# Sorting edge records by source: PE matmuls in 13 groups and 221 chunk writes in place of 832 single-record writes

## The chip, the core and the metric

The kernel runs on one core of one Trainium2 chip. The metric is the device time in microseconds of one execution, from the first to the last instruction with what lies around it; the median of three runs stands for a kernel. Engines: PE (TensorE, with PEld for its weight loads), DVE (VectorE), ACT (ScalarE), POOL (GpSimd), SP (SyncE, which here only issues DMAs).

## What is computed

Four layers of a graph network over 6250 nodes with 128 features and 106,250 edges that are sorted by destination, each followed by a residual sum and a layer norm. The layers, cut to what matters:

```python
x = ln(x + mean_by_dst(x[src]) @ W_neigh.T + b)                        # neighbour mean
x1 = relu(mean_by_dst(x[src]) @ Wl + x @ Wr + b)                       # sage 1
x_sage = relu(mean_by_dst(x1[src]) @ Wl2 + x1 @ Wr2 + b2)              # sage 2
x_gat = relu(attention over dst, 2 heads, of (x_sage @ W)[src])        # gat
x_rgcn = means by (dst, kind of edge) of (x_gat @ Wrel)[src]; x = ln(x + normalize(concat @ Wf))
ef = concat(x[row], x[col], edge_attr); h = relu(batch_norm(ef @ W1 + b1))
x = ln(x + x + segment_sum(h @ W2 + b2, row) / (count + 1))            # sums by SOURCE (row = src)
x = ln(x + (x @ W0 + segment_sum(h8[edge_type, src] * weight, dst)) / degree)
```

The edges come sorted by destination. The third layer sums by source, so the kernel needs, for every edge, a record (low part of the source, destination, two attributes) at a place that is ordered by source.

## The kernel before

**Tiles and passes.** 128 edges are a tile; T = 832 tiles, in turns of U = 16. `aggregate` is one pass over all edges, and runs six times: `block0`, `sage1`, `sage2`, `gat`, `rgcn` and, at the end, a last one. In each, POOL issues one gather per tile (L378) of the rows of the tile's sources into one of 16 message buffers; DVE builds a 128 x 128 matrix with a one for each edge at its destination's place in the window (L389, L392: the hot, made eight tiles ahead); PE multiplies the two into one of eight PSUM windows (L569, each f32 matmul stands as two records; in `block0` a second one, L572, gives the degree); DVE adds the window to the accumulator (L485). PE begins a half of eight windows only when DVE has added the half before, POOL refills a half's buffers only when PE has used them, and DVE reads a half's eight window bases into registers at its start. Each engine keeps the order in which its code is written. In `block0` two windows share a PSUM bank, and DVE's add of the first of a pair waits for PE's second; in the other passes each window has its own bank.

**Between the passes** lie the node stages `after_block0`, `after_sage1`, `after_sage2`, `after_gat` and `after_rgcn`, and `attention_terms` and `attention_softmax` between `sage2` and `gat`. Each is a block: every engine must end its part before any engine starts the next.

**Placing the edges.** In `block0` DVE also finds each edge's place in the order by source: 13 turns count how many edges of each partition fall in each of 49 blocks of sources (`count_block`, L397, a row of 832 elements each), PE sums these, and 49 times DVE masks a block, scans it for ranks and copies them (`mask_block` L402, `rank_block` L406, `place_block` L423). The table of places is `m.position`. Then POOL writes all records to DRAM with indirect DMAs, one for each tile, each of 128 records of 16 bytes: 108 in `after_block0`, 42 with `sage1` and its node stage, 165 with `sage2` and its stage, 240 in `attention_terms`, 107 in `attention_softmax`, 83 and 87 with `gat` and `rgcn` and theirs (`PLACES`; `Records`, L628, and `place_records`, L603). In `after_rgcn` SP waits for all of them (`load_when`) before it loads the first block of records, and its remaining stores of node rows stand behind that.

**By source.** `edge_hidden` gathers again, T2 = 880 tiles in the new order (L2001), and `scatter_by_source` sums them (loads at L2139). T2 is larger than T because each block of sources is filled up to whole tiles.

## Time and profile before

| what | value |
|---|---|
| median of 3 runs | 9341.97 us (9337.46 to 9349.73) |
| span of the profiled execution | 9347.3 us |
| busy: PE, DVE, ACT, POOL | 6289.6, 4856.4, 1137.4, 6808.7 us |
| mean granted PE clock, share of full | 0.68 |
| six passes over the edges | 1040 to 1052 us each |

A row of the busy table by stretches gives a stretch of the span, its length, and for each engine its busy time with the number of its records, then the granted clock of PE as a share of its upper level, the busy share of the DMA engines and their rate. A row of a timeline gives start, length, engine, line, operation and what ended the idle time before it. A group gives count, busy time and mean length of one, then the idle time of the engine ahead of these and its causes.

### The profile page before, as it was taken

The page shows a single profiled execution, that of the slowest core. Times are in us where ns is not written, and L with a number is a line of the kernel's source. Part 1 is how long each engine was busy: PE and PEld are TensorE (multiplying, and loading weights), DVE is VectorE, ACT ScalarE, POOL GpSimd, SP SyncE. Part 2 cuts the span into 40 slices and gives each one's busy share as a digit, 9 for nine tenths or more (in the row PEclk, how much of TensorE's full clock was granted, in tenths as well). Part 3 has the DMA queues.
Part 4 walks back from the last instruction along what each step waited for, and adds up shares of the span by engine and source line. Part 5 has one row for each costly group of instructions (what it writes and reads, how often), then busy time and mean ns, then how long its engine had stood idle before and what let it go on. Part 6 is the DMA issues. An engine that isn't in the chain of part 4 may idle for free. (4 is left out here: it accounts for less than half of the span.)

```text
span 9347.3 us, 137432 instructions
## 1 busy us (share of the span) xinstructions
PE 6289.6 (67%) x30105; PEld 4833.2 (52%) x30105; DVE 4856.4 (52%) x16305; ACT 1137.4 (12%) x2570; POOL 6808.7 (73%) x7484
## 2 busy tenths in 40 slices
PE   5666646666777789907888856665566658866665
PEld 5555424444566655607777644443455557634443
DVE  7776634444555535757777544445222217644445
ACT  0000100000000005800000100001222227610000
POOL 6777777777777777777777777777677767457775
PEclk7777755555666687559999955556777779965555
DMA  3212112222333332006777522212777765421211
GB/s 88 53 52 52 49 47 53 53 53 63 115 105 105 105 99 59 2 13 202 222 221 222 175 58 52 52 52 58 172 191 192 193 167 155 151 94 53 53 52 53
DMA packets 666147, 935.83 MB, mean 100 GB/s; under 512 B 276164, under 2 KB 445164, under 8 KB 665500
## 3 DMA queue, kind: packets, MB, share of 16 engines
q0 software_dynamic: 271328, 605.65, 24.3%
q1 hardware_dynamic: 295136, 324.43, 11.1%
q10 hardware_dynamic: 99548, 4.42, 0.9%
q14 instruction: 108, 0.88, 0.0%
q8 instruction: 27, 0.44, 0.0%
HBM read 790.93 MB, written 143.03 MB: 100 GB/s over the span
## 5 line engine op out<-in xcount | busy, mean ns | idle before, releaser
L569 PE MATMUL sage_window<-sage_hot,sage_message 128*128 128x128 f32 x4992 | 1438.7, 427 | 756.2 <-DMA sage_message<-t_x,all_src 315.1
L569 PEld LDWEIGHTS sage_window<-sage_hot,sage_message 128*128 128x128 f32 x4992 | 1067.3, 291 | 1127.8 <-issue 793.0
L378 POOL DMA_INDIRECT block_message<-t_rel,all_src x832 | 786.7, 946 | 424.1 <-issue 253.3
L485 DVE TENSOR_TENSOR first_acc<-first_acc,sage_window 128x128 f32 (+1 forms) x1664 | 590.4, 355 | 953.8 <-PE sage_window L569 946.8
L2001 POOL DMA_INDIRECT eh_message<-t_q,all_position x880 | 832.9, 946 | 278.1 <-issue 266.8
L378 POOL DMA_INDIRECT block_message<-in_x,all_src x832 | 791.6, 951 | 287.1 <-issue 253.0
L378 POOL DMA_INDIRECT gat_message<-t_h,all_src x832 | 791.8, 952 | 263.9 <-issue 253.0
L569 PE MATMUL gat_window<-gat_hot,gat_message 128*128 128x128 f32 x6656 | 845.7, 281 | 205.1 <-DVE gat_hot L389 116.3
L378 POOL DMA_INDIRECT sage_message<-t_x,all_src x832 | 786.4, 945 | 264.4 <-issue 253.2
L378 POOL DMA_INDIRECT rgcn_message<-t_rel,all_src x832 | 786.9, 946 | 262.1 <-issue 253.3
L378 POOL DMA_INDIRECT sage_message<-t_s,all_src x832 | 788.3, 948 | 259.9 <-issue 253.3
L569 PEld LDWEIGHTS gat_window<-gat_hot,gat_message 128*128 128x128 f32 x6656 | 782.4, 192 | 264.5 <-issue 142.8
L569 PE MATMUL block_window<-block_hot,block_message 128*128 128x128 f32 x1664 | 638.3, 487 | 409.7 <-DMA block_message<-t_rel,all_src 330.4
L569 PE MATMUL rgcn_window<-rgcn_hot,rgcn_message 128*128 128x128 f32 x1664 | 613.9, 479 | 362.3 <-DMA rgcn_message<-t_rel,all_src 296.9
L2058 PE MATMUL eh_ps<-eh_hot,eh_window 128*128 128x128 f32 x1760 | 466.3, 357 | 413.9 <-DMA eh_message<-t_q,all_position 394.0
L569 PEld LDWEIGHTS block_window<-block_hot,block_message 128*128 128x128 f32 x1664 | 416.5, 311 | 632.1 <-issue 440.1
L569 PE MATMUL block_windows<-block_hot,block_message 128*128 128x128 f32 x1664 | 482.7, 384 | 381.1 <-DVE first_acc L485 161.3
L569 PEld LDWEIGHTS rgcn_window<-rgcn_hot,rgcn_message 128*128 128x128 f32 x1664 | 415.1, 314 | 556.6 <-issue 400.3
L2031 DVE TENSOR_SCALAR_CACHE_REDUCE eh_hot<-eh_low_rows,all_column 128x128 f32<-128x128 bf16 x880 | 243.7, 342 | 857.4 <-DMA eh_low_rows<-t_low 857.1
L2058 PEld LDWEIGHTS eh_ps<-eh_hot,eh_window 128*128 128x128 f32 x1760 | 363.6, 256 | 486.3 <-issue 474.9
L569 PEld LDWEIGHTS block_windows<-block_hot,block_message 128*128 128x128 f32 x1664 | 360.0, 268 | 461.0 <-DVE block_hot L392 235.4
L392 DVE TENSOR_SCALAR sage_hot<-all_iota,all_rel 128x128 f32<-128x128 f32 x1680 | 498.4, 298 | 149.1 <-issue 149.0
(430 smaller groups left out, 10992.8 us busy)
## 6 DMA issues: line engine op xcount, KB each, us to landing
eh_window<-t_p SPq DMA_DIRECT2D x880, 64.0 KB
t_hidden<-eh_hidden SPq DMA_DIRECT2D x110, 512.0 KB
sc_rows<-t_hidden SPq DMA_DIRECT2D x110, 512.0 KB, 3.6
eh_low_rows<-t_low SPq DMA_DIRECT2D x110, 256.0 KB
t_rel<-n_h SPq DMA_DIRECT2D x49, 512.0 KB, 2.6
eh_message<-t_q,all_position POOLq DMA_INDIRECT x880
block_message<-in_x,all_src POOLq DMA_INDIRECT x832, 2.5
sage_message<-t_x,all_src POOLq DMA_INDIRECT x832, 2.5
```

Source lines behind the costliest of these rows:

```text
L378: pool.indirect_dma_start(message[u][:], None, table, bass.IndirectOffsetOnAxis(ap=index[:, it * U + u:it * U + u + 1], axis=0)).then_inc( ...
L392: ins = nc.vector.tensor_scalar(hot[:, u, :], m.iota[:], m.rel[:, t], None, ALU.is_equal)
L485: nc.vector.tensor_tensor(window, window, ps[k], ALU.add).then_inc(e.window_used, 1)
L569: last = nc.tensor.matmul(ps[k][:, b, :], message[u][:, f:f + P], hot[:, u, j * P:(j + 1) * P], start=(j == 0), stop=(j == heads - 1))
L2001: pool.indirect_dma_start(message[:, u, :], None, m.t_q, bass.IndirectOffsetOnAxis(ap=m.dst[:, it * U + u:it * U + u + 1], axis=0)).then_i ...
L2031: nc.vector.tensor_scalar(hot[:, q, e], rows, m.column[:], 0.0, ALU.is_equal, ALU.add, accum_out=m.of_source[:, bass.ds(it * U + q * QU + ...
L2058: nc.tensor.matmul(ps[q][:, e], window[:, u, :], hot[:, q, e], start=False, stop=False, skip_group_check=True)
```

## The change

The rank of an edge is found and used in another way.

- In `block0`, class `EdgeSlots` replaces the mask, scan and copy. The tiles are cut in G = 13 groups of 64. In the first 13 turns DVE compares, for eight tiles at a time, the sources' blocks with 0 to 48 (`hit`, 392 elements, bf16) and PE sums that over the partitions (`add_up`); `keep` copies the counts out. `find_starts` turns them into a first place for each group and block, once. In the remaining 39 turns (three for each group, 48 slots) DVE and PE rank eight tiles in six slots: `hit`, a matmul with a triangle, a product that picks each edge's rank, a sum over the blocks, and a matmul with the complement. The slots 0 to 23 of a group hold further steps, among them one scan and three operations on 850 elements.
- In `sage1`, class `EdgeSort` moves the records themselves. For four tiles (a quad) DVE makes in slot 4q two comparisons, `high_hot` (272 elements) and `low_hot` (512), and in slot 4q+1 the product `masked` (1088: one-hots of 68 places times four-word records). In slot 4q+3 PE multiplies them in four f32 matmuls of 272 columns (`move`), and 64 tiles make one group's sum, which DVE takes out (`keep`). The windows of `sage1` now lie in pairs in a bank, as in `block0`, which frees a bank for the sums.
- POOL then writes chunks of four records: 17 for each group, 221 in all, 51 with `sage1` and its node stage and 170 with `sage2` and its stage (four of each at the end of the pass). ACT copies ten groups out of the way in `after_sage1`. The writes, their loads and their waits in all other stages are gone.
- T2 is 896, since every group's part of a block is filled up to whole chunks. The clearing of tables is cut in seven DMAs.

```diff
-T2 = 880
+T2 = 896
...
+G = 13
+GT = T // G
+TURNS = GT // U
+BT = 8
+BATCHES = GT // BT
+CHUNK = 4
+SPAN = 68
+CHUNKS = SPAN // CHUNK
...
+WRITES = {"sage1": (0, 3 * CHUNKS), "sage2": (3 * CHUNKS, G * CHUNKS)}
+EARLY_CHUNKS = 4
...
-            if records and not places_edges:
-                pool.wait_ge(weights_in, 16 * len(loads))
-                records.write_early(pool)
+            if sorts:
+                pool.wait_ge(sort.kept, 1)
+            if chunks:
+                chunks.write_early(pool)
...
-                    if part == "count" and u % 4 == 1:
-                        count_block(it * 4 + u // 4)
...
+                    if counts is not None and u % 2 == 0:
+                        order.count(dve, counts, u // 2)
+                    if ranks is not None:
+                        order.rank(dve, ranks[0], ranks[1] * U + u)
+                    if of_sort is not None:
+                        sort.spread(dve, of_sort[0], of_sort[1] * U + u)
                     one_hot(bass.ds(it * U + u + HU, 1), (u + HU) % U)
-                    last_of_bank = u | 1 if places_edges else u
+                    last_of_bank = u | 1 if paired else u
...
+                if counts is not None:
+                    order.keep(dve, counts)
+                if of_sort is not None and of_sort[1] == TURNS - 1:
+                    sort.keep(dve, of_sort[0])
...
+                    if counts is not None and u % 2 == 1:
+                        order.add_up(pe, counts, u // 2)
+                    if ranks is not None:
+                        order.rank_up(pe, ranks[0], ranks[1] * U + u)
+                    if of_sort is not None:
+                        sort.move(pe, of_sort[0], of_sort[1] * U + u)
...
+    def hit(self, dve, tiles, k, used):
...
+        dve.wait_ge(self.hit_used[k], used)
...
+        self.nc.vector.tensor_tensor(self.hits[:, k], keys, blocks, ALU.is_equal).then_inc(self.hit_ready[k], 1)
...
+    def add_up(self, pe, g, i):
...
+        pe.wait_ge(self.hit_ready[k], g * (BATCHES // 2) + i // 2 + 1)
+        self.nc.tensor.matmul(self.ps_count[:, 0:BT * NT], self.ones[:], self.hits[:, k].rearrange("p j b -> p (j b)"), start=(i == 0),
+                              stop=(i == BATCHES - 1), skip_group_check=True).then_inc(self.hit_used[k], 1)
...
+    def rank(self, dve, n, s):
...
+        if role == 0:
+            self.hit(dve, n * GT + i * BT, k, n * half + i // 2 + G * half)
...
+        if role == 3:
+            dve.wait_ge(self.ranked, n * BATCHES + i + 1)
+            ranks = self.ps_rank[:, 0:BT * NT].rearrange("p (j b) -> p j b", b=NT)
+            tt(self.picked[:], ranks, self.hits[:, k], ALU.mult).then_inc(self.picked_ready, 1)
+        if role == 4:
+            dve.wait_ge(self.picked_ready, n * BATCHES + i + 1)
+            nc.vector.tensor_reduce(self.slot[:, bass.ds(n * GT + i * BT, BT)], self.picked[:], AX.X, ALU.add)
...
+        if role == 1:
+            pe.wait_ge(self.hit_ready[k], n * half + i // 2 + 1 + G * half)
+            nc.tensor.matmul(out, self.before[:], hits, start=False, stop=True, skip_group_check=True).then_inc(self.ranked, 1)
+        if role == 4:
+            pe.wait_ge(self.picked_ready, n * BATCHES + i + 1)
+            nc.tensor.matmul(out, self.rest[:], hits, start=False, stop=True, skip_group_check=True).then_inc(self.hit_used[k], 1)
...
+        if role == 0:
+            dve.wait_ge(self.used[k], n * (quads // 2) + q // 2)
+            tt(self.high_hot[:, k], places(SPAN), key(self.high, SPAN), ALU.is_equal).then_inc(self.hots_ready, 1)
+            tt(self.low_hot[:, k], places(P), key(self.low, P), ALU.is_equal).then_inc(self.ready[k], 1)
+        if role == 1:
+            dve.wait_ge(self.hots_ready, n * quads + q + 1)
...
+            tt(self.masked[:, k], hot, rows, ALU.mult).then_inc(self.ready[k], 1)
...
+    def move(self, pe, n, s):
...
+        if role == 3:
...
+            pe.wait_ge(self.ready[k], n * quads + q // 2 * 2 + 2)
+            for t in range(QU):
+                last = self.nc.tensor.matmul(self.ps[:, 0:SPAN * REC], self.low_hot[:, k, t], self.masked[:, k, t].rearrange("p h k -> p (h k)"),
+                                             start=(q == 0 and t == 0), stop=(q == quads - 1 and t == QU - 1), skip_group_check=True)
...
-        @block.gpsimd
-        def _(pool):
-            records.write(pool, 0, records.count)
-            records.settle(pool)
...
-                    order.load_when(sp, records)
+                    order.load(sp, 0)
```

PE in `sage1`, at the start of a turn. Before, the third and the following windows:

```order
L569 MATMUL sage1_window2<-sage1_hot,sage1_message2 128x128 [waits all_gathered2,all_hot_ready]
L564 REGISTER_ALU
L569 MATMUL sage1_window3<-sage1_hot,sage1_message3 128x128 [waits all_gathered3,all_hot_ready]
L564 REGISTER_ALU
L569 MATMUL sage1_window4<-sage1_hot,sage1_message4 128x128 [waits all_gathered4,all_hot_ready]
```

The same place in the change (`sage1_sort_ready0` counts DVE's `low_hot` and `masked`):

```order
L536 MATMUL sage1_windows1<-sage1_hot,sage1_message2 128x128 [waits all_gathered2,all_hot_ready]
L795 ISA [waits sage1_sort_kept]
L797 MATMUL sage1_ps_sort<-first_acc,sage1_sort_low_hot 128x272 [waits sage1_sort_ready0]
L797 MATMUL sage1_ps_sort<-first_acc,sage1_sort_low_hot 128x272 x3
L531 REGISTER_ALU
L536 MATMUL sage1_windows1<-sage1_hot,sage1_message3 128x128 [waits all_gathered3,all_hot_ready]
```

Four sorting matmuls and their waits have come between the windows of messages 2 and 3, which share the bank `sage1_windows1`.

DVE in `sage1`, at the same tiles. Before, from the first window's add to the second's:

```order
L485 TENSOR_TENSOR first_acc<-first_acc,sage1_window0 128x128
L392 ISA
L392 TENSOR_SCALAR sage1_hot<-all_iota,all_rel 128x128
L479 REGISTER_ALU
L481 REGISTER_ALU [waits all_window_ready]
L485 ISA [waits all_window_used]
L485 TENSOR_TENSOR first_acc<-first_acc,sage1_window1 128x128
```

In the change, from the first window's add on:

```order
L458 TENSOR_TENSOR first_acc<-first_acc,sage1_windows0 128x128
L784 ISA
L787 ISA [waits sage1_sort_hots_ready]
L787 TENSOR_TENSOR first_acc<-sage1_sort_high_hot,first_acc 128x1088
L399 ISA
L399 TENSOR_SCALAR sage1_hot<-all_iota,all_rel 128x128
L454 REGISTER_ALU [waits all_window_ready]
```

The product `masked` (written into the unused half of `first_acc`) stands ahead of the second add; the add of the third window, a few rows on, waits for the fourth.

PE in `block0`, in the turns that count. Before and in the change, from the second matmul of the first window (`setup_dst_in` stands for `hit_ready`, since semaphores' names are used again):

```order
L572 MATMUL block0_windows0<-block0_hot,all_ones 128x128
L564 REGISTER_ALU
L569 MATMUL block0_windows0<-block0_hot,block0_message1 128x128 [waits all_gathered1,all_hot_ready]
L572 MATMUL block0_windows0<-block0_hot,all_ones 128x128
L564 REGISTER_ALU
```

```order
L539 MATMUL block0_windows0<-block0_hot,all_ones 128x128
L609 ISA [waits setup_dst_ready,setup_ea_in]
L610 MATMUL block0_ps_count<-block0_hits,block0_ones_b 128x392 [waits setup_dst_in]
L531 REGISTER_ALU
L536 MATMUL block0_windows0<-block0_hot,block0_message1 128x128 [waits all_gathered1,all_hot_ready]
L539 MATMUL block0_windows0<-block0_hot,all_ones 128x128
```

A counting matmul with a wait for DVE stands ahead of every second window.

## Rows read from the trace of the kernel before

**Rows 1.** busy time by stretches: us; PE, PEld, DVE, ACT, POOL; clock, DMA share, GB/s:
```profile
33.00:1085.00 1052.00, 675.71 (x3324) 595.95 (x3324) 764.51 (x1938) 0.00 (x0) 791.62 (x832) 0.72 0.22 57
...
1239.00:2279.00 1040.00, 633.95 (x1660) 415.30 (x1660) 430.33 (x1669) 0.00 (x0) 786.25 (x832) 0.50 0.21 55
...
2344.00:3386.00 1042.00, 801.00 (x3320) 649.50 (x3320) 550.74 (x1668) 0.00 (x0) 788.32 (x832) 0.65 0.37 107
...
3620.00:4000.00 380.00, 342.37 (x2720) 220.38 (x2720) 277.81 (x633) 314.77 (x628) 286.61 (x288) 0.50 0.04 7
...
4222.00:5272.00 1050.00, 889.65 (x7024) 823.05 (x7025) 819.16 (x2650) 0.00 (x0) 791.93 (x833) 0.99 0.76 220
```

**Rows 2.** groups of the second pass (line, engine, form, count | busy us, mean ns | idle):
```profile
L378 POOL DMA_INDIRECT sage_message<-t_x,all_src x832 | 786.4, 945 | 264.4 <-issue 253.2 <-ACTq L325 11.1
...
L569 PE MATMUL sage_window<-sage_hot,sage_message 128*128 128x128 f32 x1660 | 634.2, 487 | 505.7 <-DMA sage_message<-t_x,all_src 313.8 <-DVE sage_hot L392 112.3 <-DVE first_acc L485 77.6
```

**Rows 3.** timeline (start us, length us) at the end of the first node stage:
```profile
1143.61 0.19 DVE L823 TENSOR_SCALAR all_has_edges<-n_degree 128x49 f32<-128x49 f32 x1
...
1238.82 0.34 SPq L353 DMA_DIRECT2D weights_sage_wl<-in_L_gnn_sage_Wl  x1
```

**Rows 4.** timeline, end of the attention terms and first instruction of the softmax:
```profile
3964.62 0.20 ACT L1204 COPY attention_e<-al_picked 128x8 f32<-128x8 f32 x1 [1.26 <-DVE al_picked L1243]
...
3993.80 0.36 SPq L1439 DMA_DIRECT2D softmax_spread<-t_last  x1
```

**Rows 5.** timeline of the softmax: the table's store and POOL's first gather of it:
```profile
4122.71 0.35 SPq L1441 DMA_DIRECT2D t_self<-softmax_spread  x1
...
4154.90 0.98 POOL L1434 DMA_INDIRECT softmax_rows<-t_self,all_last_edge  x1 [1.40 <-DMA t_rec<-attention_records,all_position]
```

**Rows 6.** timeline of the node stage behind the relational pass: SP's load, DVE's next:
```profile
6548.62 0.33 SPq L2497 DMA_DIRECT2D all_src_high<-t_rec  x1
...
6562.31 0.69 DVE L1867 TENSOR_TENSOR second_acc<-n_ps,second_fused_bias 128x512 f32<-128x512 f32 x1 [39.00 <-DMA t_q<-second_acc]
```

**Rows 7.** the node stage behind the second pass: POOL's writes, next stage's first DMA:
```profile
L628 POOL DMA_INDIRECT t_rec<-weights_records_sage,all_position x42: 966/972/1016, 2279.5 to 2336.7; - x42
...
2343.71 0.37 SPq L353 DMA_DIRECT2D first_sage_wl<-in_L_gnn_sage_Wl  x1
```

**Rows 8.** groups that go by T2: the gathers, and the loads behind them:
```profile
L2001 POOL DMA_INDIRECT eh_message<-t_q,all_position x880 | 832.9, 946 | 278.1 <-issue 266.8
...
L2139 SPq DMA_DIRECT2D sc_rows<-t_hidden x110: 332/333/343, 7726.8 to 8071.3; - x110
```

**Rows 9.** DVE forms by width:
```profile
L1261 DVE TENSOR_TENSOR al_product<-al_ps,al_high_hot 128x392 f32<-128x392 f32 x46 | 26.0, 566 | 21.9 <-issue 13.9 <-PE al_ps L1278 7.9
...
L1075 DVE TENSOR_TENSOR n_product<-first_sage_wg,first_sage_att 128x512 f32<-128x512 f32 x4 | 2.8, 688 | 0.1
...
565.60 1.09 DVE L498 TENSOR_TENSOR all_x<-all_x,neigh_neigh_bias 128x896 f32 x1
```

**Rows 10.** timeline of PE pairs at half clock (first pass) and full clock (node stage):
```profile
570.45 0.63 PE L569 MATMUL block_windows<-block_hot,block_message 128*128 128x128 f32 x2
...
570.87 0.63 PE L572 MATMUL block_windows<-block_hot,all_ones 128*128 128x128 f32 x2
...
571.65 0.42 DVE L485 TENSOR_TENSOR first_acc<-first_acc,block_windows 128x256 f32 x1 [1.24 <-PE block_windows L572]
...
2336.93 0.59 PE L912 MATMUL n_ps<-weights_sage_wl,first_acc 128*128 128x256 f32 x2
...
2337.36 0.59 PE L913 MATMUL n_ps<-weights_sage_wr,n_x_t 128*128 128x256 f32 x2
```

**Rows 11.** timeline of DVE in the second pass:
```profile
1503.31 0.30 DVE L392 TENSOR_SCALAR sage_hot<-all_iota,all_rel 128x128 f32<-128x128 f32 x1 [1.08 <-issue]
...
1503.62 0.29 DVE L485 TENSOR_TENSOR first_acc<-first_acc,sage_window 128x128 f32 x1
...
1503.83 0.52 DVE L392 TENSOR_SCALAR sage_hot<-all_iota,all_rel 128x128 f32<-128x128 f32 x1
```

More of the change, by code:

```diff
@@ L890, in _ @@
         def _(pool):
-            records.write_rest(pool)
+            chunks.write_rest(pool)
         @block.tensor
@@ L964, in by_half, with after_sage2 @@
     return weights.rearrange("(b k) n -> k b n", k=P)
[L967 removed]
+def after_sage2(nc, m, a, w, chunks):
     with ExitStack() as ctx:
@@ L989, in _ @@
         def _(pool):
-            records.write_rest(pool)
+            chunks.write_rest(pool)
         @block.sync
```

439 lines of the change are left out of this document (268 added, 171 removed).

## The prediction

> **What bounds the kernel now.** I read the busy table by stretches first [rows 1]. POOL has the same 786 to 792 us of work in every pass over the edges, and each such pass lasts 1040 to 1052 us, whatever PE and DVE do in it. The groups of the second pass say why: 832 gathers, 945 ns each, and 253 us of issue time between them [rows 2]; (786.4 + 253.2) / 832 = 1.25 us for one tile, so 5.00 us for four tiles and 20.0 us for sixteen. PE stands idle there for 314 us because a gathered tile has not landed. So a pass is paced by POOL, and DVE (430 of 1040 us in the second pass, 765 of 1052 us in the first) and PE (634 and 676 us) have room. What counts is whether they keep it. Between the passes POOL sets the time too wherever it still writes records while the other engines have ended [rows 3 to 7].
>
> **What goes away.** The 832 record writes cost POOL 972 ns and some 0.30 us of issue each (42 of them in 57.2 us, with the barrier at their start, 1.39 us each [rows 7]). Only those that stand alone are worth time; I go by the seams.
> - First node stage: DVE's last instruction ends at 1143.8, the next pass begins at 1238.8 [rows 3]; 108 writes fill the gap. With no POOL work in the stage, the last store of node rows must land and the engines meet; I allow 4 us. Gain 91 us.
> - Attention terms: the last copy ends at 3964.8, the softmax starts at 3993.8 [rows 4]. Gain 27 us after 2 us for the meeting.
> - Softmax: the table is stored at 4122.71 + 0.35, and some 2 us later it can be gathered; POOL starts only at 4154.90, after its 107 writes [rows 5]. Gain 30 us; the 49 gathers and DVE's end follow as they are.
> - Node stage behind the relational pass: SP's load of the sorted records is queued behind the wait for all writes, ahead of the stores of node rows; DVE stands for 39.0 us on such a store [rows 6]. With the records long written, what is left is the load itself and the stores behind it. Gain 32 us.
> - Node stage behind the attention pass: other work ends within 7 us of the writes; gain 6 us, an estimate from the same kind of seam.
> Together 186 us less.
>
> **What the 221 writes cost.** 51 stand in the stage where 42 stood: nine more at 1.28 us, and there the stage's last activation ends near the writes, so 12 us are added; the next stage now starts at 2343.7 [rows 7]. I take 13. 170 stand where 165 stood, beside PE work that ends last: 4 us. ACT's three copies of sorted rows stand ahead of its first copy in the second node stage and are covered by those writes.
>
> **T2 from 880 to 896.** Sixteen more gathers at (832.9 + 278.1) / 880 = 1.26 us give 20 us [rows 8]; the loads behind come at (8071.3 - 7726.8) / 109 = 3.16 us for eight tiles, so 6 us. Together 26 us. All these small terms: -186 + 13 + 4 + 26 = **-143 us**.
>
> **What the second pass gains in work.** Per four tiles DVE gets three products of 272, 512 and 1088 elements. DVE takes 566 ns for 392, 688 ns for 512 and 1.09 us for 896 elements [rows 9], about 1.04 ns for each further one: so 0.44, 0.69 and 1.29 us. PE gets four f32 matmuls of 272 columns, each two records. At the lower of its two levels, 1.2 GHz, two records of 128 columns are 0.42 us apart (570.45 to 570.87); at 2.4 GHz two of 256 columns take 0.43 us [rows 10]. Four times 272 columns: 3.57 us at the lower level, 1.83 us at the upper one.
>
> Taken as sums they fit: DVE's four hots and adds (0.52 us a pair [rows 11]), half of a base read of 1.08 us and 2.3 us of new work make 4.9 us of 5.00, and PE has 2.7 to 5.3 us. But they don't run side by side. The order of the rows on PE shows the four sorting matmuls ahead of the window 4q+3 and behind a wait for the masked records of the same four tiles. DVE makes these in its slot 4q+1, and its next add, of window 4q+2, needs window 4q+3, because both lie in one bank. So each of the 208 quads has a loop in it:
> - PE: wake-up 0.08, sorting 1.83 or 3.57, the pair of window 4q+3 0.21 or 0.42, and 0.36 from the pair's last start plus its share to DVE's add (571.29 to 571.65 [rows 10]): 2.5 or 4.4 us, in which DVE has only two hots and an add to do;
> - DVE from there, in starts 0.21 and 0.31 us behind each other [rows 11]: add, hot, add 0.73; the products of 272 and 512, overlapped, 0.97; hot and add 0.52; the product of 1088 in full 1.29; half a base read 0.54: 4.05 us.
> One turn is **6.5 us** at the upper level and **8.5 us** at the lower, against POOL's 5.00.
>
> Which level? PE would work 5.4 of 8.5 us, 63%. In the rows 61% goes with a granted 0.50, 90% (the attention terms) with 0.50 too, 77% with 0.65, 85% with 0.99, and the first pass, where PE works in lumps, has 0.72 at 64% [rows 1]. Here PE works in lumps of up to 5 us, so I take a quarter of the time at the upper level: 1 / (0.25 / 6.5 + 0.75 / 8.5) = 7.9, rounded to 7.8 us. 208 x 7.8 = 1622 us. Ahead of it DVE waits for the records, which SP loads behind the weights and eight clearing stores, 22 us in which no add is done; the 13 moves of a group's sum out of PSUM add 5. The pass lasts 1649 us instead of 1040: **+609 us** (bounds +339 and +755). The Trainium skill (TensorE: Matmul & The Clock Gate, "A second HAM failure mode: psum-queue depth-cycling") says that short idles between groups of matmuls make the clock alternate; the 0.65 and 0.72 of the rows are such mixtures, and by that the turn would lie between the two levels, as taken.
>
> **What the first pass gains in work.** It loses 49 blocks of mask, scan and copy and 52 counts, and gets two parts.
> - Counting, 13 turns of 16 tiles. Every second window DVE makes a product of 392 elements (0.57 us), PE adds it up ahead of the next window, and DVE's add waits for that window, again for the bank. At the lower level: 0.57 + 0.08 + matmul 0.33 (bf16, an estimate at half the f32 price per column) + two pairs 0.84 + 0.36 + add 0.34 + hot 0.31 + add 0.34 = 3.17, with a quarter of a base read 3.44; eight of them and 1.2 us for keeping the counts make 28.7 us against 20.0. At the upper level 24.1. PE works in small pieces there, so mostly the lower: +100 us (53 to 112).
> - Ranking, 39 turns or 104 batches of six windows, against 7.5 us of POOL. DVE: six hots and adds 3.9, three operations on 392 elements 1.45, three quarters of a base read 0.8, and 0.8 for the group's scan and its three products of 850 elements; the two places where DVE waits on PE behind a matmul of the ranking add 0.5 us at the upper level and 2.7 at the lower. So 7.4 to 9.65 us a batch: 0 to +222 us; at the first pass's 0.72 [rows 1] nearer to the upper end than PE's share suggests, since DVE now waits at every batch: +155.
> - The starts are found in some 30 linked steps, once: +10.
> Together **+265 us** (bounds +60 and +345).
>
> **Long loops.** The bodies are three and four turns long, 26 passes in all. A base read at a loop's start now shows 1.08 us of idle [rows 11]; a pass over a longer body may cost nothing more or up to the 6 us of a seam [rows 7]: 0 to 150, taken at 26. The Trainium skill (Runtime: NRT & Kernel Launch, "Instruction fetch mechanics") says that an engine holds two pages of instructions and that a taken branch out of them waits for a fetch; no row here shows that price, and by the upper bound the sum would be some 120 us more.
>
> **Sum.** The profiled span is 9347 us, the median of the runs 9342, so I add to the median: 9342 - 143 + 609 + 265 + 26 = 10099, **10100 us**.
>
> **Rivals.**
> - *The passes keep POOL's pace.* For it: the sums of work fit, and POOL is up to 16 tiles ahead. Against it: the loop of waits above, which no lead of POOL shortens. It decides at 5.00 us a quad, where PE's part would have to vanish behind DVE's. Then 9342 - 143, and 22 for the late start: some 9220 us, faster by 1.3%. Chance 0.09.
> - *The loop binds, but PE runs at the upper level throughout.* The 0.99 of the attention pass speaks for it, its 85% against it. 9342 - 143 + 339 + 60 = 9600 us. Chance 0.17.
> - *The lower level throughout, and costly loops.* 9342 - 143 + 755 + 345 + 50 to 100: 10350 to 10400 us. Chance 0.13.
> - *The writes are not fewer, or not off the seams.* 13 groups of 17 chunks are 221 and all stand in two stages, so no more than a little of the 186 us is open; it decides nothing here. A product of 1088 elements read through two repeated patterns could be dearer than its length: each 0.3 us is 62 us.
> The forecast has 0.61.
>
> **Range.** From the second rival with a little off its seams, 9560, to the third, 10370 us. A measurement tells 0.2% (19 us) from no change. Faster than that 0.09, within it 0.02, slower 0.89.
>
> **What would show it.** In the second pass: POOL's idle waits for PE's window (none now) of some 600 us; DVE's adds waiting on window records in each quad; starts of the masked product 7 to 8.5 us apart; granted clock 0.6 to 0.7. The first pass 1250 to 1400 us long, with a counting turn of 24 to 29 us. The stage behind it some 60 us instead of 154, the attention terms and softmax 57 us shorter together. It is wrong if DVE's product of 1088 elements and PE's sorting overlap, if the turn is under 5 us, or if the clock stands at 0.9 or more.

## The result and the profile after

The changed kernel takes 10110.73 us (median of 4 runs, 10102.03 to 10127.92) against 9340.4 us for the kernel before on the same chip: 1.0825 times as long, 95% interval 1.0809 to 1.0840. The forecast was 10100 us. The profiled execution spans 10105.8 us, 758.5 us more than the 9347.3 us of before.

Where the time went is read best from POOL's gathers, since each pass begins with one and ends soon after one. These are the rows of the gathers' line in the changed kernel: shortest, median and longest in ns, then the start of the first and of the last in us.

```profile
L384 POOL DMA_INDIRECT block_message<-in_x,all_src x832: 938/944/1837, 33.5 to 1363.2; - x167
L384 POOL DMA_INDIRECT sage_message<-t_x,all_src x832: 938/944/1897, 1435.3 to 3100.2; - x167
L384 POOL DMA_INDIRECT sage_message<-t_s,all_src x832: 942/946/1002, 3190.8 to 4230.0; - x167
L384 POOL DMA_INDIRECT gat_message<-t_h,all_src x832: 940/946/1082, 5015.3 to 6061.0; - x167
L384 POOL DMA_INDIRECT rgcn_message<-t_rel,all_src x832: 940/944/1008, 6168.2 to 7206.1; - x167
L384 POOL DMA_INDIRECT block_message<-t_rel,all_src x832: 940/944/1064, 9007.7 to 10045.3; - x167
L2172 POOL DMA_INDIRECT eh_message<-t_q,all_position x896: 940/944/1177, 7311.1 to 8434.1; - x180
```

The same rows of the kernel before:

```profile
L378 POOL DMA_INDIRECT block_message<-in_x,all_src x832: 939/946/1804, 33.0 to 1083.5; - x167
L378 POOL DMA_INDIRECT sage_message<-t_x,all_src x832: 940/945/1065, 1239.5 to 2278.2; - x167
L378 POOL DMA_INDIRECT sage_message<-t_s,all_src x832: 942/947/1005, 2344.4 to 3385.0; - x167
L378 POOL DMA_INDIRECT gat_message<-t_h,all_src x832: 942/949/1049, 4222.9 to 5270.6; - x167
L378 POOL DMA_INDIRECT rgcn_message<-t_rel,all_src x832: 940/945/1006, 5391.2 to 6430.4; - x167
L378 POOL DMA_INDIRECT block_message<-t_rel,all_src x832: 940/945/1160, 8247.7 to 9286.8; - x167
L2001 POOL DMA_INDIRECT eh_message<-t_q,all_position x880: 940/945/1124, 6584.1 to 7684.0; - x176
```

Their differences give each stage, first gather to last for a pass, last to first for what lies between:

| stretch | before, us | after, us | change | forecast |
|---|---|---|---|---|
| first pass | 1050.5 | 1329.7 | +279 | +265 |
| first node stage | 156.0 | 72.1 | -84 | -91 |
| second pass | 1038.7 | 1664.9 | +626 | +609 |
| node stage behind it | 66.2 | 90.6 | +24 | +13 |
| second sage stage, attention terms, softmax | 837.9 | 785.3 | -53 | -53 |
| node stage behind the attention pass | 120.6 | 107.2 | -13 | -6 |
| node stage behind the relational pass | 153.7 | 105.0 | -49 | -32 |
| edge network's gathers, and the loads behind | 1663.6 | 1696.6 | +33 | +26 |
| the four other passes | 4166.6 | 4160.4 | -6 | 0 |
| long loops, counted apart | | | inside the passes | +26 |

The sum is +757 against the spans' +758.5. The difference is rounding and the stretches ahead of the first gather and behind the last. (The -53 forecast is -27 -30 for the two seams and +4 for the chunks in that stretch.)

Three groups of the second pass answer to [rows 2] (line, engine, form, count | busy us, mean ns | idle us and what ended it):

```profile
L384 POOL DMA_INDIRECT sage_message<-t_x,all_src x832 | 813.5, 978 | 923.6 <-PE sage_windows L536 629.9
L797 PE MATMUL sage_ps_sort<-first_acc,sage_sort_low_hot 128*128 128x272 f32 x1664 | 732.1, 613 | 540.5 <-DVE first_acc L787 540.5
L458 DVE TENSOR_TENSOR first_acc<-first_acc,sage_windows 128x128 f32 x832 | 236.6, 284 | 739.6 <-PE sage_windows L536 739.6
```

POOL waited for nobody here before; now it waits 629.9 us for windows of PE. PE waits 540.5 us for DVE's masked records, and DVE 739.6 us for PE's windows. Two engines that each wait for the other, with neither full, are the picture of a loop. One turn of it, from the timeline (start us, length us, engine, line, idle before):

```profile
1499.88 0.29 DVE L458 TENSOR_TENSOR first_acc<-first_acc,sage_windows 128x128 f32 x1 [2.02 <-PE sage_windows L536]
...
1502.60 1.28 DVE L787 TENSOR_TENSOR first_acc<-sage_sort_high_hot,first_acc 128x1088 f32<-128x1088 f32 x1
...
1503.93 3.99 PE L797 MATMUL sage_ps_sort<-first_acc,sage_sort_low_hot 128*128 128x272 f32 x8 [2.19 <-DVE first_acc L787]
...
1507.72 1.92 PE L536 MATMUL sage_windows<-sage_hot,sage_message 128*128 128x128 f32 x8
...
1508.59 0.29 DVE L458 TENSOR_TENSOR first_acc<-first_acc,sage_windows 128x128 f32 x1 [4.11 <-PE sage_windows L536]
```

DVE adds at 1499.88, its product starts at 1502.60, PE sorts from 1503.93, the windows follow, and DVE's next add comes at 1508.59, after 4.11 us of waiting. The next product stands at 1510.56: 7.96 us for four tiles, where POOL needs 5.00. The eight sorting records took 3.99 us here and 2.10 us in the quad at 1497.33, which are the two levels of PE's clock, 1.2 and 2.4 GHz.

### The profile page after: what moved, and what is told of

It is laid out like the page before. It is cut to its first block and busy times, and to the rows that moved or that the text cites. A ratio compares the mean times of both kernels' runs of the same rounds, so it can differ in the third digit from the quotient of the medians.

```text
span 10105.8 us, 143547 instructions
## 1 busy us (share of the span) xinstructions
PE 6830.9 (68%) x32219; PEld 5310.8 (53%) x32219; DVE 5317.0 (53%) x17381; ACT 1149.4 (11%) x2599; POOL 6251.9 (62%) x6901
## 5 line engine op out<-in xcount | busy, mean ns | idle before, releaser
L384 POOL DMA_INDIRECT sage_message<-t_x,all_src x832 | 813.5, 978 | 923.6 <-PE sage_windows L536 629.9
L384 POOL DMA_INDIRECT block_message<-in_x,all_src x832 | 815.1, 980 | 543.3 <-PE block_windows L539 290.1
L797 PE MATMUL sage_ps_sort<-first_acc,sage_sort_low_hot 128*128 128x272 f32 x1664 | 732.1, 613 | 540.5 <-DVE first_acc L787 540.5
L384 POOL DMA_INDIRECT block_message<-t_rel,all_src x832 | 785.3, 944 | 426.1 <-issue 253.2
L536 PE MATMUL sage_window<-sage_hot,sage_message 128*128 128x128 f32 x3328 | 807.5, 399 | 252.3 <-DMA sage_message<-t_s,all_src 114.3
L536 PEld LDWEIGHTS sage_window<-sage_hot,sage_message 128*128 128x128 f32 x3328 | 654.5, 282 | 405.4 <-issue 247.8
L797 PEld LDWEIGHTS sage_ps_sort<-first_acc,sage_sort_low_hot 128*128 128x128 f32 x1664 | 470.9, 296 | 709.6 <-DVE first_acc L787 585.7
L458 DVE TENSOR_TENSOR first_acc<-first_acc,sage_windows 128x128 f32 x832 | 236.6, 284 | 739.6 <-PE sage_windows L536 739.6
L458 DVE TENSOR_TENSOR first_acc<-first_acc,block_windows 128x256 f32 x832 | 350.1, 421 | 436.2 <-PE block_windows L539 432.4
```

The source lines that it names most:

```text
L384: pool.indirect_dma_start(message[u][:], None, table, bass.IndirectOffsetOnAxis(ap=index[:, it * U + u:it * U + u + 1], axis=0)).then_inc( ...
L458: nc.vector.tensor_tensor(window, window, ps[k], ALU.add).then_inc(e.window_used, 1)
L536: last = nc.tensor.matmul(ps[k][:, b, :], message[u][:, f:f + P], hot[:, u, j * P:(j + 1) * P], start=(j == 0), stop=(j == heads - 1))
L797: last = self.nc.tensor.matmul(self.ps[:, 0:SPAN * REC], self.low_hot[:, k, t], self.masked[:, k, t].rearrange("p h k -> p (h k)"), start= ...
```

## Experiments on the loops

**The sorting a quad late.** A quad is four tiles. PE's sorting matmuls of quad q-1 stand where those of quad q stood, and the last quad of a group is sorted behind it.

```diff
-        if role == 3:
+        due = [q - 1] if role == 3 and q > 0 else []
+        if s == GT - 1:
+            due = due + [q]
+        for q in due:
+            k = q % 2
```

> The changed kernel, with one thing moved: in the second pass PE sorts the quad q-1 (not q) ahead of window 4q+3, and the last quad of a group behind it. The work and the output stay. Theory (the loop of waits): the masked records are then made some six slots before PE wants them, nothing in a quad waits for its own products, and the quad falls from 8.03 us to POOL's 5.0, at most 5.4 where PE is full at the lower level. The pass lasts 1060 to 1130 us instead of 1665, the kernel 9490 to 9570 us, about 9530; POOL's wait for PE's windows in it falls from 630 us to under 80. Rival (the amount of work, or the two engines disturbing each other): the same instructions run, so the time stays at 10110, within 40 us.

**The sorting a slot late.** The same with `role == 0`: quad q-1 is sorted ahead of window 4q.

> The changed kernel, with PE's sorting of quad q put one slot later: ahead of window 4q+4 instead of ahead of window 4q+3. The work and the output stay. Theory (the loop): DVE then has an add, a hot, an add and the next quad's two hots of 272 and 512 elements to do beside the sorting. From one masked product to the next: 1.28 + sorting 3.57 + two windows 0.84 + 0.36 + the add's start 0.21 = 6.3 us at the lower level; at the upper one 4.1, so POOL's 5.0. With both, 5.8 to 6.1 instead of 8.03: 9640 to 9720 us, about 9680. Rival (the amount of work): 10110, within 40 us.

**One sorting matmul of four.**

```diff
-            for t in range(QU):
+            for t in range(1):
                 last = self.nc.tensor.matmul(self.ps[:, 0:SPAN * REC], ...
```

> The changed kernel with three of the four sorting matmuls of each quad left out (three quarters of the edges are then missing from the order by source and its stages compute with blank records); DVE makes all its products as in the changed kernel, and PE sorts in the same place. Theory (the loop): the turn loses 2.7 us at the lower level or 1.4 at the upper: 5.1 to 5.8 instead of 8.03, the kernel 9560 to 9680 us, about 9610. Rival (DVE's added products bound the pass by their amount): no change, 10110 within 40 us.

Measured: 9609.86 us a quad late and 9625.06 us a slot late, beside 9344.67 us for before. Both give back the better part of the loss with every instruction still there, so the amount of work is not what bound the pass. The granted clock in it rose as well, from 0.70 to 0.85 and 0.89, and these two runs can't tell how much of the gain is the clock's. With one matmul of four the kernel took 10003.71 us, but 369 us of that lie behind the relational pass (2171 us from its last gather to the last pass, against 1802 us with the sorting a quad late), where blank records are worked on; the second pass itself fell as foretold, at a clock of only 0.55, with its masked products 5.7 us apart in the mean. The gathers of the second pass, in this order a quad late, a slot late and one of four:

```profile
L384 POOL DMA_INDIRECT sage_message<-t_x,all_src x832: 942/948/2044, 1417.4 to 2604.7; - x167
...
L384 POOL DMA_INDIRECT sage_message<-t_x,all_src x832: 940/945/2021, 1444.9 to 2635.6; - x167
...
L384 POOL DMA_INDIRECT sage_message<-t_x,all_src x832: 942/947/1895, 1425.7 to 2625.8; - x167
```

The pass lasts 1187, 1191 and 1200 us instead of 1665. From the first I had expected 1060 to 1130 us and from the kernel 9490 to 9570, and it stopped short of both; the second came out a little under its 9640 to 9720. The groups of the gathers say why, in the same order:

```profile
L384 POOL DMA_INDIRECT sage_message<-t_x,all_src x832 | 929.6, 1117 | 324.0 <-issue 253.0 <-ACTq L329 65.4 <-PE sage_windows L536 5.5
...
L384 POOL DMA_INDIRECT sage_message<-t_x,all_src x832 | 923.4, 1110 | 336.5 <-issue 250.8 <-ACTq L329 68.3 <-PE sage_windows L536 17.4
...
L384 POOL DMA_INDIRECT sage_message<-t_x,all_src x832 | 834.5, 1003 | 434.6 <-issue 224.1 <-PE sage_windows L536 142.7 <-ACTq L329 67.8
```

With the sorting a quad late POOL's wait for windows is gone (5.5 us), its issue time is the old 253 us, but a gather takes 1117 ns instead of 945: 832 x 0.172 = 143 us, and 1039 + 143 = 1182. POOL sets the pace again, at a slower pace of its own; a slot late it is nearly the same. With one matmul of four the pass has a similar length for another reason: the loop is shorter but still there, POOL waits 142.7 us for windows, and its gathers are held back less (1003 ns).

**What holds a gather back.** In the timeline of the kernel with the sorting a quad late the long gathers are those that begin inside DVE's product:

```profile
1508.57 1.29 DVE L787 TENSOR_TENSOR first_acc<-sage_sort_high_hot,first_acc 128x1088 f32<-128x1088 f32 x1
...
1509.12 1.57 POOL L384 DMA_INDIRECT sage_message<-t_x,all_src  x1 [0.30 <-issue]
...
1519.78 1.28 DVE L787 TENSOR_TENSOR first_acc<-sage_sort_high_hot,first_acc 128x1088 f32<-128x1088 f32 x1
...
1520.00 1.89 POOL L384 DMA_INDIRECT sage_message<-t_x,all_src  x1 [0.30 <-issue]
```

Both end 0.83 us behind the product (1509.86 and 1510.69; 1521.06 and 1521.89), wherever in it they began, and so do all 205 that begin in one, 0.81 to 0.85 us behind it: a gather waits until the product is done and then needs most of its time. Of the pass's 832 gathers, 205 begin in a product of 1088 elements and take 1464 ns in the mean, 86 in one of 512 (1205 ns), 62 in one of 272 (1141 ns), 92 in a hot (954 ns) and 131 in an add out of PSUM (952 ns); 243 begin with DVE idle (946 ns). Against 946 ns the three products make 106 + 22 + 12 = 140 of the 143 us.

I tested this apart from sorting, in the kernel before, with one idle DVE operation for every four tiles of the second pass. Nothing waits for its result.

```diff
+                    if phase == "sage1" and u % 4 == 1:
+                        nc.vector.tensor_tensor(spare_out[:], spare_in[:], spare_in[:], ALU.mult)
                     one_hot(bass.ds(it * U + u + HU, 1), (u + HU) % U)
```

> The kernel before with one thing added in the second pass: once per four tiles, DVE multiplies one idle tile of 1088 elements by itself (two inputs in SBUF) into another that nobody reads. No loop is made, PE gets nothing, and DVE has room: 430 us of 1040 busy, 270 more with it. Theory (with the sorting a quad late, POOL's gathers in this pass took 1117 ns instead of 948, and the long ones are those that begin while DVE makes a product of two SBUF inputs: such a product holds a gather back until it ends): a quarter of the gathers begin in a product of 1.28 us in every 5.1 and wait 0.5 us in the mean, so gathers take some 1070 ns and the pass 1140 to 1160 us instead of 1040; the kernel 9430 to 9470 us. Rival (POOL is slowed by PE's sorting, the clears of the tables or the DMA traffic): gathers stay at 945 ns and the kernel at 9345 us, within 20.

```diff
+                        nc.vector.tensor_scalar(spare_out[:], spare_in[:], m.column[:], None, ALU.is_equal)
```

> As the kernel with the idle product, but the idle DVE operation has one input tile of 1088 elements and one number per partition to compare it with (the form of the hots). Theory (two SBUF inputs are what holds a gather back): gathers stay at 945 to 955 ns, the pass at 1040 us and the kernel at 9345 us, within 20. Rival (any long DVE operation holds gathers back): as with the product, 9430 to 9470 us.

```diff
+                        nc.vector.tensor_reduce(spare_out[:, 0:1], spare_in[:], AX.X, ALU.add)
```

> As the kernel with the idle product, but the idle DVE operation is a reduction of the 1088 elements to one number per partition: one input, no factor, no second input, and about as long as the product. With the product, gathers that began in it took 1144 ns, with the compare (824 ns long) 1059 ns. Theory (it is the form of the operation that holds a gather back, not its length on DVE): gathers stay at 944 to 948 ns, the pass at 1038 to 1042 us, the kernel at 9345 us, within 20. Rival (any DVE operation of a microsecond holds a gather back): gathers at 980 to 1000 ns and the kernel at 9380 us.

> The kernel with the idle reduction once more, because the first look fell on a chip where all kernels took 25% longer and every engine stood between its instructions; there the gathers were at 948 ns. Theory (the form of the operation holds a gather back): gathers 944 to 948 ns, the pass 1038 to 1042 us, the kernel 9345 us, within 20. Rival (any DVE operation of a microsecond does): gathers 980 to 1000 ns and 9380 us.

Beside 9352.0 us for before, the product gave 9388.61 and the compare 9380.86 us. Product first, then compare, each with the operation's row and the gathers' group:

```profile
L480 DVE TENSOR_TENSOR sage_spare_out<-sage_spare_in x208: 1283/1284/1331, 1254.2 to 2320.9; 128x1088 f32<-128x1088 f32 x104
...
L380 POOL DMA_INDIRECT sage_message<-t_x,all_src x832 | 827.5, 995 | 264.4 <-issue 253.3 <-ACTq L325 11.1
```

```profile
L480 DVE TENSOR_SCALAR sage_spare_out<-sage_spare_in,all_column x208: 778/781/1025, 1252.0 to 2308.2; 128x1088 f32<-128x1088 f32 x104
...
L380 POOL DMA_INDIRECT sage_message<-t_x,all_src x832 | 817.0, 982 | 264.3 <-issue 253.2 <-ACTq L325 11.1
```

The product holds gathers back in a kernel without any sorting: 995 against 945 ns, and the kernel's 37 us are about POOL's 41 (827.5 against 786.4 in [rows 2]). It costs less than expected (a pass of 1140 to 1160 us, and it is 1080; a kernel of 9430 to 9470). The 208 gathers that begin in a product do so on average 0.32 us ahead of its end, where a random place would be 0.64 us ahead, and take 1144 ns, again the rest of the product and 0.82 us. So POOL and DVE fall into step; that they do so because a gather that is held back delays the tile that DVE waits for is my reading, not tested.

My rule of "two inputs" fell with the compare. It has one input tile and holds gathers back too, by 37 ns each. It also runs at another pace: 781 ns for 1088 elements, where the product needs 1284. 54 of the 208 are longer themselves (up to 1025 ns), all of them with a gather beginning inside, and unlike the product it also reaches gathers that began before it: the 118 that begin with DVE idle take 1087 ns in the mean. The reduction is the clean case. Both runs of it fell on chips where every kernel, the one before too, took about a quarter longer (11665 and 11546 us for before) and engines stood idle between their instructions, so their times are used only against that pair, 11673 and 11538 us; but how long a gather takes can be read:

```profile
L480 DVE TENSOR_REDUCE sage_spare_out<-sage_spare_in x208: 1271/1279/1281, 1464.8 to 2641.1; 128x1 f32<-128x1088 f32 x104
...
L380 POOL DMA_INDIRECT sage_message<-t_x,all_src x832: 938/944/1062, 1451.7 to 2632.1; - x167
```

This is the second run; 190 gathers begin in a reduction, 0.59 us ahead of its end, and take 944 ns, as long as any. In the first run it is 189 gathers at 946 ns. So it is the form of the operation, not its length. The Trainium skill (SBUF — State Buffer, "Who interferes with whom") says that VectorE and GpSimd share one pair of SBUF ports under an exclusive lock, that a tensor_tensor with both inputs in SBUF contends with a GpSimd instruction that reads SBUF, that a tensor_scalar in a two-port mode contends too and the loser then blocks for the whole instruction, and that a tensor_reduce never contends on this chip. The product's and the reduction's rows agree; the compare's do, if its faster pace is that mode. It infers that a tensor_tensor leaves the making of DMA descriptors alone; the gathers here, which read their indices from SBUF, are held back by it.

**Both passes late.** On top of the sorting a quad late, PE's matmuls of counting and ranking in the first pass are put later in the same manner, and DVE's product and sum of the ranks one slot later.

```diff
-                    if counts is not None and u % 2 == 1:
-                        order.add_up(pe, counts, u // 2)
+                    if counts is not None and u % 2 == 1 and u > 1:
+                        order.add_up(pe, counts, u // 2 - 1)
...
-        if role == 1:
+        if role == 3:
             pe.wait_ge(self.hit_ready[k], n * half + i // 2 + 1 + G * half)
...
-        if role == 4:
-            pe.wait_ge(self.picked_ready, n * BATCHES + i + 1)
+        if role == 1 and i > 0:
+            self.rank_rest(pe, n, i - 1)
```

> The kernel with the sorting a quad late, and in the first pass too every matmul of counting and ranking is put later on PE: the counts of a batch one pair of windows later, the ranks two slots later (ahead of window 6i+3), DVE's product of them one slot later, and the rest matmul three slots later (ahead of window 6i+7). The work and the output stay. Theory (loops of waits in both passes): counting needs 16 us of DVE per 16 tiles, so it falls from 28.1 us to POOL's 20.0; ranking needs 7.4 us of DVE a batch, so it falls from 9.2 us to 7.5 to 8.0. The first pass lasts 1080 to 1140 instead of 1330 us. With 9530 for the second pass alone the kernel takes 9270 to 9350 us, about 9300, and is faster than the kernel before by 0.4% or the same. Rival (amount of DVE work in the first pass): nothing of its 279 us comes back, and the time is 9530, slower than before by 2%.

Measured 9327.61 us (10 runs) against 9344.67 us (13 runs): ratio 0.9981, interval 0.9972 to 0.9991: 0.2% faster than before, next to nothing, but the whole loss is gone. The first pass's two steps, by an instruction that runs once a counting turn and one that runs once a group of 64 tiles; first the changed kernel, then this one:

```profile
L618 DVE COPY all_inv_degree<-block_ps_count x13: 557/559/560, 73.8 to 411.1; 128x392 f32 x13
...
L663 DVE TENSOR_SCALAR block_limit<-block_base x13: 181/184/240, 429.6 to 1311.3; 128x49 f32<-128x49 f32 x13
```

```profile
L622 DVE COPY all_inv_degree<-block_ps_count x13: 558/559/559, 66.1 to 308.8; 128x392 f32 x13
...
L671 DVE TENSOR_TENSOR block_shift<-block_first,block_limit x13: 202/204/228, 328.6 to 1061.3; 128x49 f32<-128x49 f32 x13
```

A counting turn falls from 337.3 / 12 = 28.1 us to 20.2, a ranking batch from 881.7 / 12 / 8 = 9.18 us to 7.63, with the same instructions. The first pass lasts 1078 us, 252 us less than in the changed kernel; the 27 us that remain over before are gathers that take longer again (820.4 us of gathers against [rows 1]'s 791.6).

**No product left in the second pass.** On top of that, the two hots are made by eight compares with one number per partition, and ACT, which has nothing to do in this pass, makes the masked records.

```diff
+            for t in range(QU):
+                tile = bass.ds(n * GT + q * QU + t, 1)
+                high = ts(self.high_hot[:, k, t], self.m.iota[:, 0:SPAN], self.high[:, tile], None, ALU.is_equal)
...
+                        last = nc.scalar.activation(self.masked[:, k, t, :, j], self.high_hot[:, k, t], ACT.Copy,
+                                                    scale=self.records[:, bass.ds(pair * 2 * QU + (k * QU + t), 1), j])
```

> The kernel with both passes' matmuls put late, and in the second pass no DVE product of two SBUF inputs is left: the two hots are made by eight compares of 68 or 128 elements with one number per partition, and ACT, which is idle in this pass, makes the masked records by sixteen activations of 68 elements with one factor per partition. The work and the output stay. Theory (the products hold the gathers back): gathers fall from 1105 to under 960 ns and the pass from 1177 to 1040 to 1060 us; the kernel takes 9190 to 9220 us, faster than before by 1.4%. ACT: 16 activations at 0.25 us are 4.0 us of a quad's 5.0. Rival (something else slows POOL): 9330 us as before this change; second rival (an activation of 68 elements costs 0.39 us, as those of 128 do): 6.2 us a quad and 9420 us.

Measured 9242.84 us (9239.96 to 9247.5) against 9352.0 us: ratio 0.9886, interval 0.9870 to 0.9903. This version is 1.1% faster than the kernel before, and so faster than both kernels. The gathers and ACT's group in it:

```profile
L388 POOL DMA_INDIRECT sage_message<-t_x,all_src x832 | 797.3, 958 | 335.6 <-issue 248.0 <-POOLq L936 61.2 <-PE sage_windows L540 26.4
...
L808 ACT ACTIVATE first_acc<-sage_sort_high_hot,first_acc 128x68 f32<-128x68 f32 x3328 | 823.2, 401 | 259.7 <-DVE sage_sort_high_hot L793 259.7
```

Gathers are at 958 ns and the pass at 1071 us, from 1177 us with both passes late. Pass and kernel missed what was expected, 1040 to 1060 us and 9190 to 9220, by 11 and 23 us. Beside the second pass of before (1039 us), 11 us are gathers that are still a little held back and 26 us are POOL's waits for windows. PE's sorting now waits for ACT's records, 219 us in all, which is the likely cause of those 26. An activation costs ACT 0.247 us of busy time, as taken (16 of them 3.96 us a quad); the 401 ns are its whole length, much of it overlapped with the next.

## Experiments on the small terms

**Seams without writes.** The kernel before with its record writes left out, and the waits for them.

```diff
-        for n in range(first, last):
+        for n in range(0):
             batch, turn = divmod(n, 16)
```

> The kernel before with all 832 record writes left out (the order by source is then blank, and the stages behind the relational pass compute with blank records); every load, rank and place of the records stays. Only the five seams ahead of the edge network are read. My terms of the prediction: first node stage 91 us shorter, attention terms and softmax 57, node stage behind the attention pass 6, node stage behind the relational pass 32, and here the first node stage behind the second pass some 30 shorter. Rival (the writes were hidden by other work, and the seams hold other waits): under 40 us together.

The edit reached less than that text says: 347 of the 832 writes, those of attention terms and softmax, are issued at another line and stayed, so this run tells nothing on these two seams. The other 485 were left out. From its gathers, the first node stage lasts 63.2 us (before 156.0), the one behind the second pass 62.2 (66.2), behind the attention pass 108.3 (120.6), behind the relational pass 103.0 (153.7): 93, 4, 12 and 51 us shorter. The writes were the seams, as forecast, but for the node stage behind the second pass, where I had said 30 and other work ends only 4 us sooner. The whole kernel took 9356.68 us beside 9352.0, since its edge network, which works on blank records here, is 178 us longer from first gather to last.

**Long bodies.** The kernel before, its plain passes in bodies of four turns.

```diff
-                with dve.Fori(0, ITERS, 1) as it:
-                    turn(it, False)
+                with dve.Fori(0, ITERS // 4, 1) as n:
+                    for r in range(4):
+                        turn(n * 4 + r, False)
```

> The kernel before with the loops of its plain passes (second, third and last pass) written as thirteen turns of a body four times as long instead of 52 of one; the instructions that run are the same. In the changed kernel DVE stands 4.0 us at each start of such a body, in which it waits for nothing that the profile shows, against 1.08 at a short one. Theory (the length of the body alone makes this): DVE and PE stand 3.5 to 4.5 us there, twelve times a pass; POOL's loop is not written so and DVE has room, so each pass stays at 1040 us and the kernel at 9345, within 20. Rival (the stall belongs to the sorting or to the move out of PSUM in the changed kernel): 1.1 us at most, and the same time.

> The kernel with bodies of four turns once more, for the same reason; on that chip the stall at a body's start could not be told from the others. Theory (the length of the body alone makes the stall): DVE stands 3.5 to 4.5 us at each start of a body in the second pass, twelve times, and the pass stays at 1040 us, the kernel at 9345, within 20, since DVE has room. Rival (it belongs to the sorting): 1.1 us at most.

In the changed kernel DVE's first instruction of a body of the second pass reads so, and twelve times stand 3.62 to 4.00 us there, 45.6 us in all:

```profile
1581.01 0.44 DVE L781 TENSOR_TENSOR sage_sort_high_hot<-all_iota,all_position 128x272 f32<-128x272 f32 x1 [4.00 <-issue]
```

Both runs of the long bodies fell on the two slow chips (11716 beside 11665 us, 11580 beside 11546). In the first the stall can't be told from others. In the second it can:

```profile
1739.16 0.29 DVE L392 TENSOR_SCALAR sage_hot<-all_iota,all_rel 128x128 f32<-128x128 f32 x1 [4.59 <-issue]
```

Twelve starts of bodies show 3.8 to 6.0 us (59.4 us together), at 64-tile distance; the kernel with the reduction, on the same chip and with short bodies, has 1.1 us at eleven of the same twelve places. So a long body makes the stall without any sorting in it. What it costs a pass with room can't be said from these chips: the kernel was 34 and 51 us slower beside its own before, where I had expected nothing, and single runs don't settle that. The Trainium skill (Runtime: NRT & Kernel Launch, "Instruction fetch mechanics") says that a taken branch out of the two pages that an engine holds waits for a fetch. The trace agrees, at some 3 us more than a short body's start.

## Why the prediction was right

- **The bound before, and the loop.** Right. The loop was in the order of the instructions before any time was known, and moving PE's sorting by one slot or one quad dissolved it, with the work unchanged.
- **The turn of 7.8 us.** My own mixture gives 7.89, which I called 7.9 and then entered as 7.8; 7.9 would have made the forecast 21 us longer. Between body starts 195 masked products stand 7.86 us apart in the mean. 157 of them are 7.7 us or more apart (mean 8.13; I had 8.5 at the lower level), 23 under 7 us (mean 6.29; I had 6.5). Both levels came out a little shorter than worked out, and the upper one took less than the quarter I gave it; the two cancel. The masked products begin 21 us behind the pass's first gather, as taken.
- **The first pass.** Right step by step: counting 28.1 us a turn (28.7 forecast), ranking 9.18 us a batch within 7.4 to 9.65, near the upper end. The +155 stood for 8.99 us, and 9.18 less the stalls of the long loops below is 8.97.
- **Long loops, 26 us.** Too small. Twelve starts in the second pass cost 2.7 us each over the 1.08 of [rows 11], 33 us. In the first pass the six repeats of the ranking's first loop, whose body also adds the bias, show 4.64 to 5.00 us, and those of its second loop 1.0; that is 22 more, so some 55 us. Since the loops of waits stand still meanwhile, I count them in full; no run has the sorting in short bodies, so this is an estimate. Why the second loop shows no stall stays open.
- **The seams.** 84, 53 and 13 us where 91, 53 and 6 were said. The node stage behind the relational pass gave 49 instead of 32: more than the 39.00 us of [rows 6], from which I had taken some off for the load itself; the run without writes shows 51. The stage behind the second pass lost 24 instead of 13. There the step failed, since in the changed kernel DVE and PE are behind POOL when the last gather is issued (the last masked product begins at 3118.1, the last gather at 3100.2), and that lag falls into this stage: with both passes late the stage is 78.6 us.
- **How much of the hit is luck.** The mechanism was right, but the hit is closer than its terms were: 757 us were forecast, and 758.5 lie between the profiled spans, 770 between the medians, in a sum with bounds of hundreds. By the count above the long loops cost 29 us more than said, and the two passes without them 24 us less (593 of 609 and 257 of 265). The weight of the two clock levels was a guess, and its two errors cancel. The stretches outside the first two passes missed by up to 17 us each and by 1 in sum, apart from 6 us in the four other passes.
- **What was missed.** The rival "the passes keep POOL's pace" was priced at 9220 us. With both loops gone the kernel takes 9328. The pace that POOL can keep is itself slower beside DVE's new products, by 143 us in the second pass and some 30 us in the first. In the changed kernel this hides behind the loop. It did not touch the forecast, but my price of the best case was wrong by 108 us, and had the kernel been written with the late order, a forecast by my sum would have missed by as much. With the products of the second pass gone too it takes 9243 us, near that price. The trace of before already had the effect, and I read past it. In its first pass seven gathers begin in the 896-element products of [rows 9]; five of them take 1.58 to 1.80 us, and each of the seven ends 0.81 to 0.85 us behind its product:

```profile
602.55 1.08 DVE L498 TENSOR_TENSOR all_x<-all_x,neigh_neigh_bias 128x896 f32 x1
...
602.87 1.58 POOL L378 DMA_INDIRECT block_message<-in_x,all_src  x1 [0.31 <-issue]
```

## What to carry to other kernels

Work added to two engines that both have room is not free when one engine's result of this step is wanted by the other within the same step. List, for each pair of engines, how many slots lie between making and using, and give every exchange more slots than its latency; here one quad of distance was worth 500 us with the same instructions. Then look at the engine that sets the pace: a GpSimd that issues gathers was slowed here by VectorE products with two SBUF inputs and by a long compare, however much room the sums of work seemed to leave. Splitting such a product into forms that leave the gathers alone, and giving part of it to an idle engine, paid here (the pass from 1177 to 1071 us) though it took more instructions; which of the two did how much was not tested.

## What the runs showed of the hardware

- A gather of 945 ns that begins inside a DVE tensor_tensor of 1088 elements with both inputs in SBUF ends 0.81 to 0.85 us behind that operation (205 gathers with the sorting a quad late); beside a tensor_reduce of the same length it takes 944 ns, and beside a DVE add that reads one input from PSUM 952 ns.
- TensorE's granted clock does not go by its busy share in these passes. Second pass of the version with ACT's masks (window us, its length, PE, PEld, DVE, ACT and POOL busy, then the clock):

```profile
1170.00:2242.00 1072.00, 676.22 (x3308) 545.80 (x3308) 687.60 (x3346) 817.98 (x3308) 796.98 (x832) 0.93 0.21 55
```

  PE is 63% busy there at a granted 0.93; before it was 61% busy at 0.50 [rows 1]. In between lie the changed kernel's pass (60%, 0.70) and the one with the sorting a quad late (69%, 0.85). No run here says what makes the difference. With the higher clock PE's busy time in the pass grew from 634 us [rows 1] only to 676 us here and 816 us with the sorting a quad late, with all the sorting added.
